# The selective scan of a two-layer image kernel: products with C of two steps in one GpSimd instruction, and seven of the 24 products with B on GpSimd

## What is computed

```python
x_dbl = jnp.einsum('bkdl,kcd->bkcl', xs, x_proj_weight)
dts, Bs, Cs = jnp.split(x_dbl, [R_RANK, R_RANK + N_STATE], axis=2)
dts = jax.nn.softplus(einsum(dts, dt_projs_weight) + dt_projs_bias)
A = -jnp.exp(A_logs)                      # (4, 192, 16)
def step(h_prev, t):                      # over the 3136 positions
    dA = jnp.exp(dt_t[..., None] * A)
    dBx = (dt_t * x_t)[..., None] * B_t[:, :, None, :]
    h = dA * h_prev + dBx
    y = jnp.einsum('bkdn,bkn->bkd', h, C_t)
```

## Time and profile before

| | us |
|---|---|
| median of three executions | 23417.88 |
| lowest and highest of them | 23393.66, 23420.24 |
| the profiled execution | 23412.67 |
| its span, first to last instruction | 23410.9 |

### The profile page before, as it was taken

The page is one execution under the profiler, slowest core; times in us unless marked ns, Lnnn a source line. Parts: engine busy times, 40 slices in busy tenths (PEclk is TensorE's granted clock), DMA queues, the critical chain, the costliest instruction groups (busy, mean ns, idle before and its releaser), DMA issues. The chain is left out here.

```text
span 23410.9 us, 290956 instructions
## 1 busy us (share of the span) xinstructions
PE 17671.3 (75%) x83608; PEld 6368.3 (27%) x83608; DVE 19513.2 (83%) x21619; ACT 9356.7 (40%) x14503; POOL 16923.9 (72%) x9092
## 2 busy tenths in 40 slices
PE   8999999997777677777777777777777777777731
PEld 5556555552222111111111111111111111111111
DVE  5555555556666899999999999999999999999976
ACT  3333333334444344444444444444444444444420
POOL 0000000007888899999999999999999999999977
PEclk9999999998777676777677677767766776677665
DMA  0000000004555555555555555555555555555556
GB/s 17 15 15 14 14 14 14 14 14 148 184 178 181 140 118 121 119 122 117 116 121 122 121 116 118 122 121 120 118 117 120 121 122 117 116 121 122 119 135 166
DMA packets 918185, 2417.28 MB, mean 103 GB/s; under 512 B 61030, under 2 KB 270440, under 8 KB 901680
## 3 DMA queue, kind: packets, MB, share of 16 engines
q1 hardware_dynamic: 917040, 2404.95, 45.2%
HBM read 1897.33 MB, written 507.38 MB: 103 GB/s over the span
## 5 line engine op out<-in xcount | busy, mean ns | idle before, releaser
L1162 POOL TENSOR_TENSOR c_pr<-c_hs,c_c_u 128x784 f32<-128x784 f32 x6144 | 11216.7, 1847 | 749.4 <-DVE c_hs L1126 749.4
L1069 ACT ACTIVATE c_psum<-c_dt_u,c_a_neg 128x784 f32<-128x784 f32 x6144 | 5641.6, 918 | 8506.4 <-DVE c_hs L1126 8458.7
L1014 PE MATMUL c_psum<-c_pr,c_red 128*64 128x392 f32 x24576 | 7519.3, 728 | 0.0
L1126 DVE TENSOR_TENSOR_SCAN c_hs<-c_psum,c_carry,c_dbx 128x784 f32<-128x784 f32 x3456 | 6272.7, 1845 | 0.0
L1003 PE MATMUL c_psum<-c_br_u,c_sel 48*128 48x512 bf16 (+1 forms) x9216 | 3210.5, 441 | 3994.8 <-DVE c_dbx L1106 3888.7
L1106 DVE TENSOR_TENSOR c_dbx<-c_u_u,c_psum 128x784 f32<-128x784 f32 x4608 | 4390.2, 953 | 55.4 <-PE c_psum L1003 55.4
L177 POOL TENSOR_TENSOR a_xpb<-a_x_sb,a_pb_sb 98x768 f32<-98x768 f32 x128 | 231.0, 1804 | 5059.8 <-DVE a_x L262 5048.7
L1151 POOL TENSOR_TENSOR c_dbp<-c_u_u,c_bp_u 128x784 f32<-128x784 f32 x1536 | 2858.7, 1861 | 45.0 <-DMA c_c_u<-scr_bc 45.0
L1003 PEld LDWEIGHTS c_psum<-c_br_u,c_sel 48*128 48x128 bf16 x9216 | 557.3, 102 | 8494.5 <-DVE c_dbx L1106 7963.1
L1014 PEld LDWEIGHTS c_psum<-c_pr,c_red 128*64 128x64 f32 x24576 | 1807.9, 181 | 3522.1 <-issue 2286.9
L1126 DVE TENSOR_TENSOR_SCAN c_hs<-c_psum,c_carry,c_dbp 128x784 f32<-128x784 f32 x1152 | 2133.1, 1852 | 0.0
(11 more groups left out here) (104 smaller groups left out, 17976.1 us busy)
## 6 DMA issues: line engine op xcount, KB each, us to landing
c_c_u<-scr_bc SPq DMA_DIRECT2D x512, 1568.0 KB, 26.9
c_dt_u<-scr_dt SPq DMA_DIRECT2D x512, 588.0 KB, 7.4
c_u_u<-scr_u SPq DMA_DIRECT2D x512, 588.0 KB, 10.8
c_bp_u<-scr_bc SPq DMA_DIRECT2D x512, 392.0 KB, 20.2
scr_dt<-p_dt_o SPq DMA_DIRECT2D x128, 1176.0 KB, 9.6
scr_u<-p_u_o SPq DMA_DIRECT2D x128, 1176.0 KB, 7.2
scr_y<-c_y_sb SPq DMA_DIRECT2D x256, 294.0 KB, 14.4
d_yin<-scr_y SPq DMA_DIRECT2D x32, 2352.0 KB, 14.4
```

The costliest lines, as they stand in the source:

```text
L1014: mm = pe.matmul(Y(3 * w + q)[64 * h:64 * h + 64, :], red[:], pr[:, s % RP, HT * h:HT * h + HT], start=(p == 0 and opens(w)), stop=(p == N ...
L1069: nc.scalar.activation(dA(s), dt_u[:, d, s // NPR, :], ACT.Exp, scale=a_neg[:, k, s:s + 1]).then_inc(exp_done, 1)
L1126: nc.vector.tensor_tensor_scan(hs[:, s % RH, way], dA(s)[:, way], data, init, ALU.mult, ALU.add).then_inc(scan_done, 1)
L1162: nc.gpsimd.tensor_tensor(pr[:, s % RP, :], hs[:, s % RH, :], c_u[:, d, s % NPR, :], ALU.mult).then_inc(prod_done, 1)
```

## The change

POOL forms the products with C of steps s and s + 1 (s even) in one instruction of 128 x 2 x 784, which waits for both scans and frees both slots at once. POOL takes seven products with B instead of six: those of steps 3, 7, 11, 13, 15, 19, 23; the product of step s + 7 stands behind the pair s, s + 1. bp_u holds three pairs of states (3, 5, 7) instead of two, so its two DMAs per unit carry three rows for two. DVE does 17 products with B instead of 18, and TensorE spreads B 17 times.

```diff
-POOL_PAIRS = (3, 7)
-DVE_PAIRS = tuple(p for p in range(NPR) if p not in POOL_PAIRS)
+POOL_PAIRS = (3, 5, 7)
+POOL_STEPS = (3, 7, 11, 13, 15, 19, 23)
+DVE_STEPS = tuple(s for s in range(3 * NPR) if s not in POOL_STEPS)
...
-                                 rows(32 * d)[:, h, POOL_PAIRS[0]::4, :].to_broadcast([64, 2, CT])).then_inc(u_in[d], 16)
+                                 rows(32 * d)[:, h, POOL_PAIRS[0]::2, :].to_broadcast([64, 3, CT])).then_inc(u_in[d], 16)
...
-                if s % NPR in POOL_PAIRS:
+                if s in POOL_STEPS:
                     return
...
-                    for s in range(STEPS):
+                    for s in range(0, STEPS, 2):
                         n = STEPS * v + s
-                        pool.wait_ge(scan_done, n + 1)
-                        after(pool, red_done, n - RP + 1)
-                        nc.gpsimd.tensor_tensor(pr[:, s % RP, :], hs[:, s % RH, :], c_u[:, d, s % NPR, :],
-                                                ALU.mult).then_inc(prod_done, 1)
-                        if s % 4 == 1:
-                            i = s // 4 + 1
-                            if i < len(POOL_STEPS):
-                                times_b(b, w, i)
-                            elif w + 1 < WI:
+                        pool.wait_ge(scan_done, n + 2)
+                        after(pool, red_done, n - RP + 2)
+                        nc.gpsimd.tensor_tensor(pr[:, s % RP:s % RP + 2, :], hs[:, s % RH:s % RH + 2, :],
+                                                c_u[:, d, s % NPR:s % NPR + 2, :], ALU.mult).then_inc(prod_done, 2)
+                        if s + 7 in POOL_STEPS:
+                            times_b(b, w, POOL_STEPS.index(s + 7))
+                        elif s + 7 - STEPS == POOL_STEPS[0]:
+                            if w + 1 < WI:
                                 times_b(b, w + 1, 0)
                             elif not last:
                                 times_b(b + 1, 0, 0)
```

More of the change, by code:

```diff
@@ L881, in build_scan @@
     STEPS = 3 * NPR
-    MULS = 3 * len(DVE_PAIRS)
+    MULS = len(DVE_STEPS)
     RH, RP, RB, RG = 6, 8, 4, 2
@@ L928, in unit_of @@
             return o, (c if d == 0 else NCHK - 1 - c), d
-        DVE_STEPS = [s for s in range(STEPS) if s % NPR in DVE_PAIRS]
-        POOL_STEPS = [s for s in range(STEPS) if s % NPR in POOL_PAIRS]
         @block.sync
```

## The result

The changed kernel takes 23,201.1 us (median of four, 23,180.7 to 23,202.9) against 23,417.8 before (23,393.7 to 23,420.2): ratio 0.9907, 95% interval 0.9891 to 0.9922. Forecast were 23,194. The profiled executions are 23,178.9 and 23,410.9 us in span, 232.0 apart; the medians are 216.7 apart, the forecast said 224.

A forecast was written before the change was run, and what follows sets the result against it. DVE was taken to bound the scan stage, with POOL close behind. 23,412.7 - 228 (removed product) + 2 + 2 (last pair, first load) = 23,189, put on the median 23,194 us; range 23,165 to 23,320.

The forecast's parts named there:

- DVE sets the pace and POOL stays behind it: Scan stage: after the change DVE's unit takes 56.4 us and POOL's 55.9, so DVE stays the bound; chance 0.80.
- The price of the removed product: Step 13's product with B leaving DVE saves 0.89 us per unit, 228 us over 256 units.
- The pair: POOL's joined product with C for two steps, taken at 3.61 us, that is, no gain from joining.
- the far one: Upper end for POOL's joined product: 4.17 us, at 2.66 ns a column from a strided 96x3136 instruction.
- the margin between 3.61 and 3.65: POOL's joined product, taken at 3.61 us, could last up to 3.65 with DVE still the bound.
- The waits of the pair: POOL's joined product waits for the second scan; its lag of 3.8 us fits the six-slot hs ring's 5.1 us reserve.
- the crowded steps: POOL's five joined and four B products take 25.3 us against 22.7 for DVE's ten steps: up to 2.6 us lag.
- part 4: TensorE at its lower clock: weight loads wait never over 0.6 us for POOL, far below a scan's 1.75; no cost.
- The loads: Larger bp_u loads: 392 KB more per unit, 1.9 us of transfer under 13 us of cover; 2 us once at the start.
- The signs named in advance: Trace signs of being right: instruction counts, joined products of 3.45 to 3.65 us, POOL waiting 0.5 to 2.5 us a unit, loads 56.8 apart.
- The rivals with POOL as the bound: POOL's joined product lasts 3.66 to 3.71 us (23,320 at 3.69; chance 0.06), or from 3.73 loses (24,780 at 4.17; chance 0.06).

The follow-up runs named there:

- with eight products: Changed kernel (products with C joined) with an eighth product with B, that of step 21, on POOL: 23,095.2 us, ratio 0.9858.

## Why the prediction was right

**DVE sets the pace and POOL stays behind it**: right. DVE is full, POOL waits, and both parts taken alone do what the two sums say.

**The price of the removed product**, 0.89 us by the distance between starts: 0.88 to be read in the trace. The product's own duration, 0.95, would have given 243 us. The seventh product alone gave ratio 0.9906, 220 us.

**The pair**: taken at 3.61, it is 3.46. The term was mis-sized by 0.15 us per pair, on the safe side, and it did not enter the sum. Of the two ends, the far one (2.66 ns per column of the strided 3136-column instruction) was no guide at all: the pair takes 2.21. The estimate from the Trainium skill (GPSIMD Engine Reference, Performance versus the Vector engine), 3.44 us, was within 0.02 of it. The forecast leaned on the margin between 3.61 and 3.65 more than was needed: the margin was 0.19.

**The waits of the pair**: right, and too careful. With a pair of 3.46 the crowded steps make 5 x 3.46 + 4 x 1.80 - 22.7 = 1.8 us of lag instead of 2.6, and units without a carry none (54.1 against 55.3). The kernel with seven single products, with POOL's unit at the 55.9 of the forecast, showed DVE stopped for 4.6 us in all. The pair's own wait, for two scans, was not tried apart from the joining. On TensorE's side the reserve was read too narrowly: its weight loads waited up to 2.6 us for a pair, where part 4 had 0.6 and a limit of 1.75, and DVE still never waited for a spreading but at the start.

**The loads**: covered, as said, for the data themselves. Missed was the store of y behind them: its landing moved by 3.4 us, of which about 2.0 go with the larger loads, and ScalarE waited 46 us for it. It did not reach DVE, so the sum stands; with eight products it did, for 100 us. The forecast had asked only when the loaded data are needed, not who else waits for a DMA behind them. Loads of two units in turn started 57.15 us apart (15082.58 - 15025.43), not 56.8: they follow POOL's last product, whose lag differs from unit to unit. Over four units they start (15251.10 - 15025.43) / 4 = 56.42 apart, the forecast's average of 56.41:

```profile
15025.43 1.81 SPq L944 DMA_DIRECT2D c_dt_u<-scr_dt  x2
...
15045.12 1.50 SPq L961 DMA_DIRECT2D scr_y<-c_y_sb  x2
15082.58 1.39 SPq L944 DMA_DIRECT2D c_dt_u<-scr_dt  x2
...
15251.10 1.29 SPq L944 DMA_DIRECT2D c_dt_u<-scr_dt  x2
```

**The signs named in advance**: 4352 products on DVE and 3072 pairs and 1792 products on POOL, pairs in 3.45 to 3.65 (3.48 to 3.59), four steps at 9.61 us as before, 22 us of idle time before scans where under 50 was the sign, POOL idle before pairs for 2.2 us per unit (553 / 256, of which the profile gives 467 to scans). All seen but the distance of the loads, which holds on average only. The rivals with POOL as the bound were right as mechanisms and did not apply here: they set in with an eighth product without joining, or a ninth with it.

**Where the joining's gain went**: with the joining alone POOL's waiting grew by 441 us and the time stayed. In this change the joining buys nothing; the seventh product on POOL is the whole of it. It pays only together with an eighth.

## What to carry to other kernels

Where two engines run side by side with rings between them, add up each one's work per unit by distances between starts, and take the longer: moving an instruction is worth its distance on the busy engine, once, until the sums cross. Making the second engine faster is worth nothing by itself; it buys room to move more, so try the next step too. And when a load grows or starts later, look at the stores issued behind it.

## What was not expected of the hardware

- A part of about 0.15 us in each of POOL's products that does not grow with the columns: 1.805 us for 784 columns, 3.46 for 1568, so 2.11 ns a column and the rest fixed, if the cost is linear between these two widths, the only ones tried. The same for an operand read twice by a broadcast (3.53 us).
- A ring of six slots kept two engines apart with 0.5 us of slack in 56.4, in a stage of 14.5 ms, with 4.6 us of stops in all.
- With eight single products, where POOL never waited, its rows lengthened and the distance of their starts did not: a product with C lasts 2790 ns on average, and the starts below are still 1.80 us apart. There a duration is no price.

```profile
15005.78 2.70 POOL L1149 TENSOR_TENSOR c_dbp<-c_u_u,c_bp_u 128x784 f32<-128x784 f32 x1
15007.58 4.50 POOL L1160 TENSOR_TENSOR c_pr<-c_hs,c_c_u 128x784 f32<-128x784 f32 x2
```
